# Inverse norms of queries and keys: from one power per half tile to a seed from exponent bits and two Newton steps

## The reference

```python
qkv = x @ Wqkv[i]                       # 16 heads of 64
q = l2norm(q) * qs                      # t / max(norm(t), 1e-12) along the 64
k = l2norm(k) * ksc
q = q * cos * scale + rotate_half(q) * sin * scale
k = k * cos / scale + rotate_half(k) * sin / scale
out = local_attention(q, k, v)          # window 32: own and previous block
x = out @ Wo + x
x = ffn(x) + x                          # layer norm, W1, a * gelu(gate), W2
```

## Time and profile before

| | us |
|---|---|
| median of three runs (lowest, highest) | 2024.64 (2019.8, 2025.11) |
| the profiled execution, its own time | 2023.72 |
| its span, from first to last instruction | 2021.9 |
| PE busy in the span | 1896.6 |
| POOL busy in the span | 1669.2 |
| ACT busy, DVE busy | 1593.2, 1555.0 |

### The profile page before, as it was taken

How to read it: one execution, slowest core, us unless ns; L and a number is a source line. 1 busy time by engine, 2 the same in 40 slices (tenths; PEclk the granted TensorE clock), 3 DMA queues, 4 the chain that set the end, 5 groups by cost and what they waited for, 6 DMA issues and landing times.

```text
span 2021.9 us, 67246 instructions
## 1 busy us (share of the span) xinstructions
PE 1896.6 (94%) x22192; PEld 1437.1 (71%) x22192; DVE 1555.0 (77%) x4021; ACT 1593.2 (79%) x5612; POOL 1669.2 (83%) x1264
## 2 busy tenths in 40 slices
PE   7997999989999989999988999998999999999997
PEld 5665777765777765777764777774777775777773
DVE  5786888867888866888866888866888876888876
ACT  6775888876888875888875888885888885888883
POOL 3326999986999986999985999985999995999971
PEclk9997999999999999999999999999999999999999
DMA  3002111112111112211112112212211111111110
GB/s 122 14 11 66 48 47 47 47 43 77 48 47 47 47 43 76 51 47 47 47 43 63 49 47 55 52 34 73 49 47 47 47 48 38 49 47 47 47 46 21
DMA packets 44547, 99.42 MB, mean 49 GB/s; under 512 B 7345, under 2 KB 24209, under 8 KB 43505
## 3 DMA queue, kind: packets, MB, share of 16 engines
q1 hardware_dynamic: 44400, 97.59, 18.5%
HBM read 19.59 MB, written 1.05 MB: 10 GB/s over the span
## 4 chain that ended last, share of the span: by engine, by line
PE 80%; ACT 8%; issue 6%; DVE 3%; POOL 2%; DMA 0%; DVEq 0%; ACTq 0%; SPq 0%; POOLq 0%
PE bank L1198 10%; PE bank L1211 9%; PE bank L1246 8%; PE bank L1225 8%; PE bank L1191 8%; PE bank L1227 6%; PE bank L1232 6%; PE bank L1226 6%; PE bank L1182 3%; ACT kT L548 3%; PE bank L1328 3%; ACT prob L510 2%; PE bank L1317 2%; PE bank L1315 2%; PE bank L1238 2%
## 5 line engine op out<-in xcount | busy, mean ns | idle before, releaser
L345 POOL TENSOR_TENSOR rn<-n2c,half_neg 128x8 f32<-128x8 f32 x384 | 636.7, 1658 | 93.2 <-DVE n2c L837 92.5
L510 ACT ACTIVATE prob<-bank,nmax 128x96 f32<-128x96 f32 x1536 | 501.2, 350 | 133.7 <-DVE nmax L787 133.4
L347 POOL TENSOR_TENSOR tsum<-tc_,ts_ 128x512 f32<-128x512 f32 x384 | 489.6, 1275 | 0.0
L350 POOL TENSOR_TENSOR w_nat<-tsum,rn 128x512 f32<-128x512 f32 x384 | 400.5, 1043 | 37.7 <-POOL tsum L347 15.1
L830 DVE TENSOR_REDUCE n<-nat 128x8 f32<-128x512 f32 x384 | 262.6, 684 | 150.4 <-ACT nat L526 139.8
L510 ACT ACTIVATION_READ_ACCUMULATOR prob<-bank,nmax 128x1 f32 x1536 | 331.5, 216 | 7.0 <-issue 7.0
L787 DVE TENSOR_REDUCE nmax<-bank 128x4 f32<-128x384 f32 x384 | 196.3, 553 | 152.7 <-PE bank L1191 152.7
L1198 PE MATMUL bank<-idf,prob 128*96 128x128 f32 x1536 | 245.6, 283 | 46.9 <-ACT kT L548 30.1
L519 ACT ACTIVATE pT<-bank 96x512 f32<-96x512 f32 x384 | 230.4, 600 | 74.6 <-PE bank L1198 72.6
L840 DVE TENSOR_TENSOR ts_<-bank,ropeL 128x256 f32<-128x256 f32 x768 | 286.2, 414 | 0.0
L1225 PE MATMUL bank<-w_hi,xs 128*128 128x512 f32 x576 | 277.5, 482 | 3.7 <-DVE xs_lo L819 2.3
(11 more groups left out here) (125 smaller groups left out, 3311.2 us busy)
## 6 DMA issues: line engine op xcount, KB each, us to landing
vspace<-v_nat SPq DMA_DIRECT2D x96, 384.0 KB, 4.0
vspace<-v_nat SPq DMA_DIRECT2D x96, 256.0 KB, 3.4
vspace<-v_nat SPq DMA_DIRECT2D x95, 128.0 KB, 2.3
nat<-w_qkv SPq DMA_DIRECT2D x5, 1536.0 KB, 8.6
wo<-w_o SPq DMA_DIRECT2D x6, 512.0 KB, 4.0
w<-w SPq DMA_DIRECT2D x6, 341.0 KB, 3.1
shared<-w_qkv SPq DMA_DIRECT2D x1, 1536.0 KB, 11.1
w<-w SPq DMA_DIRECT2D x6, 192.0 KB, 3.1
```

The source lines that it names most:

```text
L345: nc.gpsimd.tensor_tensor(rn[:, r, :], n2c[:, r, :], half_neg[:, 0:8], ALU.pow).then_inc(pool_step, 1)
L347: nc.gpsimd.tensor_tensor(tsum[:, r, :], tc_[:, r, :], ts_[:, r, :], ALU.add).then_inc(pool_step, 1)
L350: nc.gpsimd.tensor_tensor(w_nat[:, r, :].rearrange("p (h d) -> p h d", d=D), tsum[:, r, :].rearrange("p (h d) -> p h d", d=D), rn[:, r, :] ...
L510: last = nc.scalar.activation(prob[:, 4 * b + i, :], SB[b][:, i * SPAN:(i + 1) * SPAN], ACT.Exp, bias=nmax[:, p, 8 * G + 4 * b + i:8 * G + ...
```

## The change

The loop over tiles 1 to 15 of every layer gets the inverse norms in another way; tile 0 of a layer (`rotate_first`) keeps the power. For each pair of halves (j = 0 and 1, then 2 and 3) ACT makes one seed, an Exp of the squared norms read as integers, with a scale and a bias. POOL then refines the 16 values by two Newton steps, eight `tensor_tensor` instructions on 128x16 that each wait for the one before, and only then multiplies either half. DVE writes `n2c` after `ts_` instead of before. PE's code is unchanged.

```diff
-            def rotate(q_idx):
-                for j in range(4):
-                    r, Q = j % 2, q_idx + j
-                    eng.wait_ge(n2c_ready, Q + 1)
-                    nc.gpsimd.tensor_tensor(rn[:, r, :], n2c[:, r, :], half_neg[:, 0:8], ALU.pow).then_inc(pool_step, 1)
-                    eng.wait_ge(pj_dve, Q + 1)
-                    nc.gpsimd.tensor_tensor(tsum[:, r, :], tc_[:, r, :], ts_[:, r, :], ALU.add).then_inc(pool_step, 1)
-                    eng.wait_ge(pool_step, Q * 2 + 2)
-                    at_least(eng, tp_full, Q - 1)
-                    nc.gpsimd.tensor_tensor(w_nat ... tsum ... rn ..., ALU.mult).then_inc(w_ready, 1)
+            def rotary_sum(t, j):
+                at_least(eng, w_ready, Q - 1)
+                eng.wait_ge(pj_dve, Q + 1)
+                nc.gpsimd.tensor_tensor(tsum[:, r, :], tc_[:, r, :], ts_[:, r, :], ALU.add).then_inc(sum_ready, 1)
+            def refine(t, g, seeds):
+                eng.wait_ge(seeded, seeds)
+                nc.gpsimd.tensor_tensor(rn_a[:, :], s2, rn0[:, g, :], ALU.mult).then_inc(refined, 1)
+                eng.wait_ge(refined, K + 1)
+                nc.gpsimd.tensor_tensor(rn_b[:, :], rn_a[:, :], rn0[:, g, :], ALU.mult).then_inc(refined, 1)
...
+                nc.gpsimd.tensor_tensor(rn[:, :], rn_c[:, :], rn_z[:, :], ALU.mult).then_inc(refined, 1)
+            def rotate(t, seeds):
+                rotary_sum(t, 0)
+                rotary_sum(t, 1)
+                refine(t, 0, seeds)
+                rotated(t, 0)
+                rotary_sum(t, 2)
+                rotated(t, 1)
+                rotary_sum(t, 3)
+                refine(t, 1, seeds + 1)
+                rotated(t, 2)
+                rotated(t, 3)
@@ ACT
+            def seed(t, g):
+                eng.wait_ge(n2c_ready, t * 4 + (2 * g + 2))
+                at_least(eng, refined, (t * 2 + g) * 8 - 8)
+                nc.scalar.activation(rn0[:, g, :], n2c ... .bitcast(mybir.dt.int32), ACT.Exp,
+                                     scale=LOG_SCALE, bias=log_bias[:, 0:1]).then_inc(seeded, 1)
                         probs_out(t, 0, 1, 4)
+                    if not closing:
+                        seed(t + 1, 0)
                     exps(t, p, 1, 0)
...
                     heads_out_T(t, 0, 4)
+                    if not closing:
+                        seed(t + 1, 1)
@@ DVE, rotary
+                at_least(eng, sum_ready, Q - 1)
                 nc.vector.tensor_tensor(tc_ ...)
-                eng.wait_ge(n2_ready, Q + 1)
-                nc.vector.tensor_reduce(n2c[:, r, :], n2[:, r, :, :], AX.X, ALU.max).then_inc(n2c_ready, 1)
                 for a in range(2):
...
                 last.then_inc(pj_dve, 1)
+                eng.wait_ge(n2_ready, Q + 1)
+                at_least(eng, refined, (t * 2 + j // 2) * 8)
+                nc.vector.tensor_reduce(n2c[:, r, :], n2[:, r, :, :], AX.X, ALU.max).then_inc(n2c_ready, 1)
```

More of the change, by code:

```diff
@@ L1 @@
+import math
 import concourse.bass as bass
@@ L26 @@
 EPS = 1e-5
+SCALE2 = 0.5 ** (1 / 3)
+SCALE1 = (0.5 * SCALE2) ** (1 / 3)
+STEP = (1.5 * SCALE2 / SCALE1 * (1 + 1.68e-4), 1.5 / SCALE2)
+LOG_SCALE = -0.5 * math.log(2.0) / 2 ** 23
+LOG_BIAS = 0.5 * math.log(2.0) * (127 - 0.0430) + math.log(SCALE1)
 QK_AT, V_AT = [0, 1, 2, 4], [3, 5]
@@ L101, in build @@
         n2c = sb("n2c", [P, 2, 8])
-        rn = sb("rn", [P, 2, 8])
+        rn0 = sb("rn0", [P, 2, 2 * 8])
+        rn = sb("rn", [P, 2 * 8])
+        rn_a, rn_b, rn_c, rn_z = (sb(n, [P, 2 * 8]) for n in ("rn_a", "rn_b", "rn_c", "rn_z"))
+        step_c = sb("step_c", [P, 2, 2 * 8])
+        log_bias = sb("log_bias", [P, 1])
         tc_ = sb("tc_", [P, 2, HB])
@@ L337, in _ @@
             pow_norm(0, 3)
-            eng.wait_ge(init_done, 9)
-            def rotate(q_idx):
+            nc.gpsimd.memset(step_c[:, 0, :], STEP[0]).then_inc(init_done, 1)
+            nc.gpsimd.memset(step_c[:, 1, :], STEP[1]).then_inc(init_done, 1)
+            nc.gpsimd.memset(log_bias[:, :], LOG_BIAS).then_inc(init_done, 1)
+            eng.wait_ge(init_done, 12)
+            def rotary_sum(t, j):
+                Q, r = t * 4 + j, j % 2
+                at_least(eng, w_ready, Q - 1)
+                eng.wait_ge(pj_dve, Q + 1)
+                nc.gpsimd.tensor_tensor(tsum[:, r, :], tc_[:, r, :], ts_[:, r, :], ALU.add).then_inc(sum_ready, 1)
@@ new lines, in rotated @@
+            def rotated(t, j, first=False):
+                Q, r, g = t * 4 + j, j % 2, j // 2
+                eng.wait_ge(sum_ready, Q + 1)
+                eng.wait_ge(refined, (t * 2 + g) * 8 + (4 * r + 4 if first else 8))
+                at_least(eng, tp_full, Q - 1)
+                nc.gpsimd.tensor_tensor(
+                    w_nat[:, r, :].rearrange("p (h d) -> p h d", d=D), tsum[:, r, :].rearrange("p (h d) -> p h d", d=D),
+                    rn[:, r * 8:r * 8 + 8].rearrange("p (h o) -> p h o", o=1).to_broadcast([P, 8, D]), ALU.mult).then_inc(w_ready, 1)
@@ L342, in rotate, with rotate_first @@
+            def rotate(t, seeds):
[9 more added lines that the diff above has]
+                rotated(t, 3)
+            def rotate_first(t):
                 for j in range(4):
-                    r, Q = j % 2, q_idx + j
+                    r, Q = j % 2, t * 4 + j
@@ L355, in split_keys @@
+                    nc.gpsimd.tensor_tensor(rn[:, r * 8:r * 8 + 8], n2c[:, r, :], half_neg[:, 0:8], ALU.pow).then_inc(refined, 4)
+                    rotary_sum(t, j)
+                    rotated(t, j, True)
             def split_keys(t, p):
@@ L403, in _ @@
             nc.gpsimd.memset(vw[0:WIN, 0, 0, :], 0.0).then_inc(vw_ready, 1)
-            rotate(0)
+            rotate_first(0)
             def layer(l, last):
                 with eng.Fori(1, TILES) as n:
-                    rotate((n + l * TILES) * 4)
+                    rotate(n + l * TILES, n * 2 + l * (2 * TILES - 2) - 1)
                 for s in range(SUPERS):
@@ L421, in layer @@
                 if not last:
-                    rotate((l + 1) * TILES * 4)
+                    rotate_first((l + 1) * TILES)
             with eng.Fori(0, DEPTH - 1) as l:
@@ L526, in square @@
                 nc.scalar.activation(sq[:, j % 2, :], PJ[QK_AT[j] % 2][:, :], ACT.Square).then_inc(pj_act, 1)
+            def seed(t, g):
+                eng.wait_ge(n2c_ready, t * 4 + (2 * g + 2))
+                at_least(eng, refined, (t * 2 + g) * 8 - 8)
+                nc.scalar.activation(rn0[:, g, :], n2c[:, :, :].rearrange("p r h -> p (r h)").bitcast(mybir.dt.int32), ACT.Exp,
+                                     scale=LOG_SCALE, bias=log_bias[:, 0:1]).then_inc(seeded, 1)
             def values(t, p, j):
@@ L825, in rotary @@
                 eng.wait_ge(pj_act, t * 6 + (QK_AT[j] + 1))
-                if not (fresh and j < 2):
-                    at_least(eng, w_ready, Q - 1)
                 heads3 = "p (h d) -> p h d"
```

16 lines of the change are left out of this document (15 added, 1 removed).

## The result

The changed kernel takes 2708.66 us (median of four runs, 2705.12 to 2711.67), the kernel before took 2024.88 in the same job (2019.8 to 2028.26). The ratio is 1.338, with a 95% interval from 1.334 to 1.341: slower by a third, 684 us. The forecast was 2690 us with a range from 2510 to 2890.

The account below looks back on a forecast made before the run. PE and POOL were taken as equally full, with products used just in time; the new order makes them late. Span 2021.9 + 529 for tiles + 135 for clock + 3 for layer beginnings = 2689, forecast 2690 us, range 2510 to 2890.

Parts of the forecast that it names:

- A step (s): One chained POOL step on 128x16 with its semaphore handover: 0.30 us, bounds 0.27 to 0.56, sixteen per tile.
- The rival of dear steps: Dispatch and register work make POOL's steps cost more: 2830 us at 0.40 per step, 3065 at 0.56; chance 17%.
- POOL off the path: POOL swaps four powers for sixteen steps, 1.8 us per tile lighter, but none of this is on the path.
- First wait: PE's transposes of (t+1, 0) wait about 3.9 us for POOL's product, 10.59 us after those of (t, 2), before 6.70.
- Second wait: PE's transposes of (t+1, 2) wait 1.8 to 2 us, starting 11.53 us after those of (t+1, 0).
- Tiles: A loop tile takes 22.12 us against 16.24 without the clock; over 90 tiles 529 us more.
- The clock: PE's clock falls when it waits, slowing work up to projection 4: 1.5 us per tile, bounds 0 to 2.3, 135 us.
- Covers: ACT's seed, perhaps 0.3 us, is hidden by other work; DVE's `n2c` wait for the first refinement costs nothing more.
- the openings of layers: `rotate_first` gets `n2c` 0.7 us later, six times: at most 4 us, taken as 3.

Follow-up runs that it names:

- filling the wait: Changed kernel with 30 throwaway transposes on PE into an idle bank ahead of the transposes of (t+1, 0): 2550.27 us, ratio 1.261.
- power in the new order: Changed kernel, POOL's order kept, with one power on 128x16 per pair in place of seed and eight steps: 2907.76 us, ratio 1.438.
- both late moves: Changed kernel with PE's transposes of (t+1, 0) put beside those of (t+1, 1): 2384.15 us; with (t, 2) also put beside (t, 3): 2197.64 us.
- norms sooner: Changed kernel, PE untouched, `n2c` ahead of `ts_`, seeds earlier, POOL doing sum, steps, product, sum, product per pair: 2424.7 us, ratio 1.197.
- the fitted version: Changed kernel with earlier `n2c` and seeds, one sum before the steps, and PE's transposes (t+1, 0) just ahead of projection 4: 2101.11 us, ratio 1.040.
- the best version: The fitted version with DVE's `xs_lo` put behind the rotary of half 3: 2078.18 us, ratio 1.026.
- the kernel before with PE's move alone: Kernel before, powers kept, with only PE's transposes of (t+1, 0) moved to just ahead of projection 4: 2045.75 us, ratio 1.011.

## Why the prediction was right, by its own steps

- **A step (s).** Put at 0.30 us, bounds 0.27 and 0.56. Measured 0.223 with 0.08 of handover, 0.30, and by the run with one Newton step each costs 0.32 us of the kernel's time. The rival of dear steps is gone.
- **POOL off the path.** It became 3.0 us per tile less busy and 1.8 less occupied, as worked out, and that gave nothing. With the old order, where twice as many steps on half the columns fill it, the loss is only 154 us.
- **First wait.** Put at 3.9 us, and (t, 2) to (t+1, 0) at 10.59. Measured 3.66, and 10.53 and 10.41. The step in the sum that was a little too large is the handover behind the sum: the first step starts 0.04 us before the sum's recorded end, not 0.08 after it.
- **Second wait.** Put at 1.8 to 2 us and at 11.53 between the two transposes. With the clock kept up it was 11.42 and 11.32, and the wait is 1.4 to 1.9.
- **Tiles.** 529 us were forecast without clock. The measured 684 less the 158 that filling the wait gave back is 526, and since the 158 are a lower bound, that is an upper one. Such closeness is in part luck: the parts err by 0.1 to 0.3 us per tile.
- **The clock.** Put at 1.5 us per tile, 135 us. Filling the wait gave back 1.76 and 158, and PE's busy time grew by 203. This is the term that was mis-sized, by 23 us at least, and by 68 if all of PE's added busy time counts. I had taken it from the earlier trace rows, 3.4 us at the lower level in the shorter case; here it is 5.0 in one tile and 3.4 in the next, and projection 4 comes 5.17 us (754.50 to 759.67) or 4.25 behind the transposes instead of 2.94 in the earlier trace rows, 1.8 more on the mean. The rule of the Trainium skill on "HAM oscillation" (TensorE: Matmul & The Clock Gate), that a loop with an idle phase begins each pass at the lower clock, held for the first of the two tiles above to the letter, and for the second from 1.4 us behind the wait on.
- **Covers.** The seed takes 0.30 us and its second is ready 0.1 us before the first step needs it (764.45 and 764.55); doubling both changed nothing that could be measured. DVE's wait of `n2c` for the refinement is 34.9 us in all and lies beside PE's wait, as argued; no run takes it away alone, so that is read from the trace and not shown. (The later place of `n2c` behind `ts_` stood in the run with Newton steps in the old order too, and is within its 154 us.) The 3 us for the openings of layers were not tested either.

The profile after has the signs that the prediction named: waits at two of four transposes that end with a product, 47.45 us for two tiles (47 forecast), POOL busy for 50.66 us in 96, some 25 us in these, and the clock at 0.89 over the same stretch:

```profile
700.00:796.00 96.00, 73.14 (x831) 58.70 (x830) 52.57 (x134) 60.88 (x211) 50.66 (x96) 0.89 0.13 33
```

What failed were expectations of the experiments: six of twelve were missed by 60 us or more (power in the new order, Newton steps in the old, both late moves, norms sooner, the fitted version), and two more by 16 and 23. In four of them I moved a wait and did not ask what the next engine in the circle would then ask for: the product of half 1 behind the sum of half 2, the seed behind ACT's last copy, the square of the second half.

What stays open: the last 32 us between the best version (2078.18) and the kernel before with PE's move alone (2045.75), where POOL still waits 207.3 us for seeds; and why the power in the new order brings 109 us of slower matmuls with only 82 us more of waits. Which part of the new order costs what (the second sum ahead of the steps, or norms that wait for both halves) no run parts either.

## What to carry to other kernels

Where an engine's results are taken just in time, what counts is when its first result comes out, and not how much it has to do: batching two halves took three microseconds of work per tile off POOL and made each result of the first half wait for the second. Before merging work into pairs, write down for the first result of a pair what now stands ahead of it, and when its reader asks for it. And where an in-order reader begins to wait in every pass, price its clock too: here at least 158 of the 684 us lost.

## What the runs showed of the hardware that was not expected

Two of DVE's operations in SBUF, the scaling of `kT` and the subtraction into `xs_lo`, are stretched when POOL's sums and products over 512 columns run beside them. In the kernel before, where a product runs beside `kT` in most tiles (from 607.77 to 608.81, with `kT` from 608.00 on):

```profile
L840 DVE TENSOR_TENSOR ts_<-bank,ropeL 128x256 f32<-128x256 f32 x768 | 286.2, 414 | 0.0
...
L812 DVE TENSOR_SCALAR kT<-kT,follows 128x256 f32<-128x256 f32 x96 | 85.8, 894 | 0.0
```

and after, where POOL stands idle then (it is idle from 756.77 to 763.31, with `kT` from 758.38 on):

```profile
L909 DVE TENSOR_TENSOR ts_<-bank,ropeL 128x256 f32<-128x256 f32 x768 | 285.7, 413 | 0.0
...
L885 DVE TENSOR_SCALAR kT<-kT,follows 128x256 f32<-128x256 f32 x96 | 34.4, 358 | 0.0
```

The same instruction on `kT` takes 0.894 and 0.358 us, and 0.717 in the fitted version, while `ts_`, which reads a bank of PSUM, stays at 0.41. So does the sum of squares into `n2`, which reads SBUF, at 0.68 in all three, also where a product runs beside it throughout. It is thus not SBUF as such. The change thus made DVE 51 us shorter there, off the path. `xs_lo` does the same the other way round, 0.301 before, 0.283 after and 0.604 in the fitted version, where a product runs beside it. In the kernel before it lies beside a power, and that does not stretch it. With the Newton steps in the old order POOL is full too, and `kT`, beside the short steps, takes 0.375 us. The Trainium skill, GPSIMD Engine Reference, section 1 (Specifications), has the two engines share their interfaces to SBUF, with contention for those DVE instructions that are in a 2-port perf mode or have two SBUF inputs. The trace agrees in that `xs_lo` has two such inputs and the sum of squares one; which of the two conditions applies to `kT` no run here shows.

The power on POOL takes 1.009, 1.658 and 2.909 us for 4, 8 and 16 columns (the earlier trace rows and the run of it), 0.16 us per column and 0.36 fixed. A chained multiplication takes 0.204 for 8 and 0.222 for 16, and the handover 0.08 in either case: a power of 8 columns is worth six such steps (1.658 / 0.28), one of 16 columns ten (2.909 / 0.30).
